# Tensor product of a graph network layer: VectorE's work on the pack before moved between the product groups of a pack's second step, and the index loads issued one turn earlier

## The chip, the core and the metric

The kernel runs on one core of a Trainium2 chip. That core has TensorE (PE in the profile, its weight loads PEld), VectorE (DVE), ScalarE (ACT), GpSimd (POOL) and SyncE (SP), which run side by side and wait for each other by semaphores. The metric is the device time of one execution in microseconds. Three runs of the kernel before took 8627.51, 8630.15 and 8634.26 us; the median is 8630.15.

## The reference

A two-layer graph network on 12,500 nodes with 32 features and 400,000 edges, sorted by their destination. The first layer is an attention over the edges, the second a tensor product:

```
h = max(layernorm(x), 0)
x = x + attention(h)                       # layer 0: q, k, v of 4 heads, softmax over a node's edges
h = max(layernorm(x), 0)                   # 8 scalars and 8 vectors per node
R = relu(weight * w1 + b1) @ w2 + b2       # per edge: 384 radial weights
Y = spherical_harmonics(edge_attr)         # per edge
msg[e, o] = sum over u, v, i: R[e, u, v, k] * Y[e, f] * h[src[e], v, i] * C[o, f, i]
x = x + (h + sum of msg over the edges of each destination)
```

Everything here concerns `msg` and the sum over edges. For it an edge's source row `h[src]` is gathered, its vectors are turned into a frame along the edge, multiplied by the radial weights and summed over the 16 inputs, and turned back.

## The kernel before

The edges are padded to 128 x 3132: each of the 128 partitions holds 3132 edges ("slots") in order. The tensor product (`tensor_product`) works on packs of 18 slots, 174 packs in all; 3 packs are a chunk, 6 packs (two chunks) are one pass of the loop body, and a pack is one *turn* `j` of it. Each engine has its own instruction stream, written out by hand in its function; there is no scheduler. What stands in these streams, and the semaphores, set the order.

For each pack:

- GpSimd gathers the 18 source rows of each partition with 18 indirect DMAs (`feat<-scratch_h,src`, line 993) into one of three buffers. At a pack's start it waits for `feat_free`, which VectorE counts up once it has used the rows, and at a chunk's start for the index list `src_i[b]`, which ACT loads (line 1123).
- VectorE *rotates* the vectors (line 1209, three instructions) and forms the *operands* (line 1218, three).
- TensorE computes the radial weights in six *weight groups*, of three slots each (lines 1008 and 1009, six matmuls a group, `radial`), into two alternating PSUM buffers `psR`. Group g waits until VectorE's product of group g - 2 is done (line 1005's wait on `prod_done`), because it overwrites its buffer.
- VectorE multiplies a group by the operands (line 1241, three instructions a group, the *product*). Products 0 to 2 are a pack's first step, 3 to 5 its second. Behind each step stands a *fold* (line 1250) that adds a few of the 16 inputs, so that TensorE has fewer to sum.
- TensorE sums a step's products over the inputs with an identity matrix (lines 1020 and 1023, the *sum*). The last matmuls of a sum (line 1023) wait for the fold.
- ACT evicts the sum from PSUM into `red` (line 1082), and prepares seeds, flags and frames (lines 1089, 1091, 1059).
- VectorE, one turn later, does the *rotations back* (line 1258, three), *additions back* (copy of line 1267, additions of lines 1269 and 1270) and *scans* (line 1279, four), which run the sums along the edges of a node. ACT stores the result (lines 1098 and 1100).

TensorE's queue is, for a pack: groups 2, 3, 4, 5; first sum; groups 0 and 1 of the next pack; second sum. It works through it in order, so group 5, which waits for product 3, holds up the first sum behind it.

VectorE's queue in a turn is: products 0 to 2, fold, products 3 to 5, fold, rotations back, additions back, scans (of the pack before), rotate, operands (of the pack behind).

Of the kernel before, what the change touches and what calls it, by code (L numbers as in the profile page):

```python
# [883 lines left out]
def tensor_product(nc, a, k):  # L884
# [11 lines left out]
    with ExitStack() as ctx:  # L896
# [41 lines left out]
        with nc.Block(no_gpsimd_drain=True) as block:  # L938
# [107 lines left out]
            def _(act):  # L1046
# [61 lines left out]
                def body(i, first, last):  # L1108
                    for j in range(TURN):
# [11 lines left out]
                        if j % PACKS == PACKS - 1 and not last:  # L1121
                            b = j // PACKS
                            act.dma_start(src_i[b][:, :], sources[:, bass.ds(i * (2 * T) + (b + 2) * T, T)]).then_inc(src_loaded[b], 16)
# [12 lines left out]
            def _(vec):  # L1136
# [87 lines left out]
                def products(i, j, s, first):  # L1224

                    q = i * (TURN * SPP) + j * SPP + s
                    r = (j * SPP + s) % 2
                    if not (first and j == 0):
                        vec.wait_ge(sum_ready, q - 1)
                    if s == 0:  # L1230
                        vec.wait_ge(turned_ready, i * TURN + j + 1)
                    for third in range(GROUPS):
                        g = GROUPS * s + third
                        ts = slice(g * TRI, (g + 1) * TRI)
                        vec.wait_ge(radial_ready, i * (TURN * GPP) + j * GPP + g + 1)
                        to = prod[r][:, third * TRI:(third + 1) * TRI, :, :]
                        for lo, n, frm in ((0, 2 * VU, 0), (2 * VU, VU, 256), (3 * VU, VU, 256)):
                            x = max(0, lo // VU - 1)
                            if s == 0 and third == 0 and x == 1:
                                vec.wait_ge(turned_copied, i * (TURN * 2) + j * 2 + 2)  # L1240
                            v.tensor_tensor(to[:, :, :, lo:lo + n], psR[:, g % 2, :, frm:frm + n * JC].rearrange("p t (j u) -> p t j u", j=JC),  # L1241
                                            ops[j % 2][:, ts, x * JC:(x + 1) * JC].rearrange("p t (j o) -> p t j o", o=1).to_broadcast([P, TRI, JC, n]),
                                            ALU.mult).then_inc(prod_done, 1)
# [42 lines left out]
                def body(i, first, last):  # L1286
                    step = chain(vec, vec_done, base + i * (TURN * per_pack) - (0 if first else of_finish))
                    for j in range(TURN):
                        begun, more = not (first and j == 0), not (last and j == TURN - 1)
                        products(i, j, 0, first)  # L1290
                        fold(i, j, 0)
                        products(i, j, 1, first)
                        fold(i, j, 1)
                        if begun:
                            rotate_back(step, i, j - 1, 0 if more else 1)
                            add_back(step, i, j - 1)
                            scan(step, i, j - 1)
                        if more:
# [151 lines left out]
```

## Time and profile before

| | |
|---|---|
| median of three runs | 8630.15 us |
| the profiled execution's own time | 8642.33 us |
| its span, first to last instruction | 8640.3 us |
| PE busy | 3594.6 us (42%) |
| DVE busy | 5311.7 us (61%) |
| POOL busy | 6479.9 us (75%) |
| ACT busy | 1921.1 us (22%) |
| first and last start of the tensor product's gathers | 4409.2 and 8465.1 us |

Times are those of one profiled execution. The share of busy time is over the whole span, of which the tensor product is a little under half; in the other half TensorE hardly works.
### The profile page before, as it was taken

How to read it: one execution, taken by the hardware profiler on the slowest of the kernel's cores; microseconds unless marked ns; L12 is line 12 of the kernel's file. 1: busy time of each engine (PE TensorE's matmuls, PEld its weight loads, DVE VectorE, ACT ScalarE, POOL GpSimd, SP SyncE). 2: the span in 40 equal slices, each digit the busy share in tenths (PEclk: the TensorE clock that was granted, in tenths of full speed). 3: DMA queues.
4: the chain of work that ended last, by engine and by line, in shares of the span. 5: the costliest groups of instructions: out<-in, count | busy, mean ns of one | idle time of the engine just before them, and what ended most of it. 6: DMA issues, size and time to landing. Idle time of an engine off the chain costs nothing. (4 is left out here: it accounts for less than half of the span.)

```text
span 8640.3 us, 61009 instructions
## 1 busy us (share of the span) xinstructions
PE 3594.6 (42%) x15884; PEld 2458.9 (28%) x15884; DVE 5311.7 (61%) x7917; ACT 1921.1 (22%) x2576; POOL 6479.9 (75%) x6677
## 2 busy tenths in 40 slices
PE   1000000000000000000048888888888888888882
PEld 0000000000000000000035655556555656655651
DVE  3233333343333433334369999999999999999993
ACT  0123332223322233222201111111111111111110
POOL 7777777777777777777667777777777777777775
PEclk6555555555555555555579999999999999999996
DMA  7333444334443444443222222222222222222221
GB/s 301 102 107 109 116 113 122 107 109 114 113 124 107 110 112 114 122 111 110 63 52 70 68 66 67 69 68 66 67 70 68 66 68 70 66 68 66 70 66 29
DMA packets 364374, 796.10 MB, mean 92 GB/s; under 512 B 143582, under 2 KB 209998, under 8 KB 344638
## 3 DMA queue, kind: packets, MB, share of 16 engines
q1 hardware_dynamic: 99880, 491.45, 19.3%
q0 software_dynamic: 213216, 166.16, 10.3%
q10 hardware_dynamic: 51126, 136.22, 4.2%
q8 instruction: 125, 2.05, 0.1%
q14 instruction: 27, 0.22, 0.0%
HBM read 499.72 MB, written 293.61 MB: 92 GB/s over the span
## 5 line engine op out<-in xcount | busy, mean ns | idle before, releaser
L993 POOL DMA_INDIRECT feat<-scratch_h,src x3132 | 3102.2, 990 | 975.1 <-issue 954.7
L537 POOL DMA_INDIRECT kv<-scratch_kv,src_i x3132 | 2971.9, 949 | 959.8 <-issue 959.8
L1020 PE MATMUL psS<-prod,ident 128*128 128x288 f32 x7656 | 1986.2, 417 | 0.7 <-ACT red L1082 0.7
L1241 DVE TENSOR_TENSOR prod<-psR,ops 128x384 f32<-128x384 f32 (+1 forms) x3132 | 1919.6, 682 | 82.7 <-PE psR L1009 47.3
L804 PE MATMUL psA<-ident,tail 128*36 128x128 f32 x3 | 0.8, 413 | 3936.5 <-DVEq L829 3936.5
L1020 PEld LDWEIGHTS psS<-prod,ident 128*128 128x128 f32 x7656 | 1505.0, 198 | 423.4 <-issue 14.1
L1008 PE MATMUL psR<-whigh,stack 128*128 128x384 f16 x3132 | 1066.8, 341 | 540.7 <-DVE prod L1241 531.1
L804 PEld LDWEIGHTS psA<-ident,tail 128*36 128x36 f32 x3 | 0.3, 127 | 3936.7 <-DVEq L829 3936.6
L1009 PE MATMUL psR<-wlow,capped 128*128 128x384 f16 x3132 | 1067.7, 342 | 0.0
L689 DVE TENSOR_TENSOR qk<-psQ,kv 128x1728 f32<-128x1728 f32 x58 | 113.6, 1958 | 1473.7 <-DMA kv<-scratch_kv,src_i 1473.7
L1082 ACT ACTIVATE red<-psS,scales 128x288 f32<-128x288 f32 x348 | 174.6, 502 | 2388.7 <-PE psS L1023 2388.3
L674 DVE TENSOR_TENSOR_SCAN psQ<-psQ,qseed 128x1760 f32<-128x1760 f32 x58 | 222.2, 3832 | 591.6 <-ACT qseed L566 591.6
L1008 PEld LDWEIGHTS psR<-whigh,stack 128*128 128x128 f16 x3132 | 312.8, 100 | 938.3 <-DVE prod L1241 753.0
L1023 PE MATMUL psS<-prod,ident 128*128 128x288 f32 x1740 | 478.9, 406 | 0.0
L1209 DVE TENSOR_TENSOR parts<-feat,psF 128x432 f32<-128x432 f32 x519 | 282.4, 599 | 173.1 <-DMA feat<-scratch_h,src 173.1
L585 ACT ACTIVATE psD<-decay 128x1980 f32<-128x1980 f32 x58 | 107.4, 1851 | 1205.2 <-DVEq L700 1205.2
L1009 PEld LDWEIGHTS psR<-wlow,capped 128*128 128x128 f16 x3132 | 316.4, 101 | 202.6 <-issue 25.4
L682 DVE TENSOR_TENSOR low<-psD,high 128x1728 f16<-128x1728 f32 x116 | 227.1, 1958 | 216.1 <-ACT high L577 203.3
L1023 PEld LDWEIGHTS psS<-prod,ident 128*128 128x128 f32 x1740 | 330.6, 190 | 91.3
L1218 DVE TENSOR_REDUCE ops<-parts 128x144 f32<-128x432 f32 x522 | 306.1, 642 | 42.1 <-DVE parts L1209 42.1
L592 ACT ACTIVATE out<-sums 128x1944 f32<-128x1944 f32 x58 | 219.9, 3792 | 468.4 <-DVEq L708 468.4
L1250 DVE TENSOR_TENSOR prod<-prod 128x864 f32<-128x864 f32 x348 | 316.1, 908 | 11.9
(254 smaller groups left out, 4039.3 us busy)
## 6 DMA issues: line engine op xcount, KB each, us to landing
w_row<-in_wT SPq DMA_DIRECT2D x116, 864.0 KB
stack<-scratch_hid SPq DMA_DIRECT2D x174, 576.0 KB
scratch_state<-out ACTq DMA_DIRECT2D x58, 1080.0 KB
kv<-scratch_kv,src_i POOLq DMA_INDIRECT x3132
qin<-scratch_qexp SPq DMA_DIRECT2D x58, 864.0 KB, 4.5
scratch_hid<-high SPq DMA_DIRECT2D x116, 432.0 KB, 11.1
scratch_hid<-low SPq DMA_DIRECT2D x116, 432.0 KB, 12.0
feat<-scratch_h,src POOLq DMA_INDIRECT x3132
```

Source lines behind the costliest of these rows:

```text
L537: nc.gpsimd.indirect_dma_start(kv[b][:, t, :], None, a["kv"], bass.IndirectOffsetOnAxis(ap=src_i[b][:, t:t + 1].bitcast(U32), axis=0)).the ...
L674: step(v.tensor_tensor_scan(flat(qrun), flat(qrun), flat(qseed), 0.0, ALU.mult, ALU.add))
L682: v.tensor_tensor(low[:, cols], units, high[:, cols], ALU.subtract).then_inc(split_done, 1)
L993: nc.gpsimd.indirect_dma_start(feat[h][:, t, :], None, a["h2"], bass.IndirectOffsetOnAxis(ap=src_i[b][:, h * PACK + t:h * PACK + t + 1].bi ...
L1008: nc.tensor.matmul(psR[:, g % 2, t, 0:384], stack[:, slot, at:at + P], whigh[:, :], start=True, stop=False)
L1009: last_mm = nc.tensor.matmul(psR[:, g % 2, t, 0:384], capped[:, slot, at:at + P], wlow[:, :], start=False, stop=True)
L1020: nc.tensor.matmul(into, ident[:, :], prod[r][:, :, j, :], start=(n == 0), stop=False)
L1023: last_mm = nc.tensor.matmul(into, ident[:, :], prod[r][:, :, j, :], start=False, stop=(j == FOLDS[s] - 1))
L1209: step(v.tensor_tensor(parts[:, :, n, :].rearrange("p t (i u) -> p t i u", i=3), f[:, :, VU:D].rearrange("p t (i u) -> p t i u", i=3), at[ ...
L1218: add_up = lambda n: v.tensor_reduce(ops[j % 2][:, :, n * JC + VU:(n + 1) * JC], parts[:, :, n, :].rearrange("p t (i u) -> p t u i", i=3), ...
L1241: v.tensor_tensor(to[:, :, :, lo:lo + n], psR[:, g % 2, :, frm:frm + n * JC].rearrange("p t (j u) -> p t j u", j=JC), ops[j % 2][:, ts, x ...
L1250: v.tensor_tensor(prod[r][:, :, 0:FOLDS[s], :], prod[r][:, :, 0:FOLDS[s], :], prod[r][:, :, JC // 2:JC // 2 + FOLDS[s], :], ALU.add).then_ ...
```

## The change

The function `products`, which did a step's three products, becomes `product` for one group; its waits and instructions are the same. In VectorE's turn the work for the pack before no longer stands behind the second fold as one block. Rotations back stand between the first fold and product 3, additions back between products 3 and 4, scans between 4 and 5, and rotate comes ahead of the second fold, with the operands behind it. On ACT the load of the next index list is issued in the turn `j % 3 == 1` of a chunk in place of `j % 3 == 2`.

```diff
-                        if j % PACKS == PACKS - 1 and not last:
+                        if j % PACKS == PACKS - 2 and not last:
                             b = j // PACKS
                             act.dma_start(src_i[b][:, :], sources[:, bass.ds(i * (2 * T) + (b + 2) * T, T)]).then_inc(src_loaded[b], 16)
...
-                def products(i, j, s, first):
+                def product(i, j, g, first):
...
+                    s, third = g // GROUPS, g % GROUPS
...
-                        products(i, j, 0, first)
+                        for g in range(GROUPS):
+                            product(i, j, g, first)
                         fold(i, j, 0)
-                        products(i, j, 1, first)
-                        fold(i, j, 1)
                         if begun:
                             rotate_back(step, i, j - 1, 0 if more else 1)
+                        product(i, j, GROUPS, first)
+                        if begun:
                             add_back(step, i, j - 1)
+                        product(i, j, GROUPS + 1, first)
+                        if begun:
                             scan(step, i, j - 1)
+                        product(i, j, GROUPS + 2, first)
                         if more:
                             rotate(step, i, j + 1)
+                        fold(i, j, 1)
+                        if more:
                             operands(step, i, j + 1)
```

VectorE's queue in one turn, before, from the first fold on (9x96 is the first fold, 9x64 the second; a product is a row of 48x16 and one of 48x8 x2; `back` are the rotations back, `seed` and `run` additions back and scans):

```order
L1250 TENSOR_TENSOR prod<-prod 128x9x96 [waits prod_done]
L1241 TENSOR_TENSOR prod<-psR,ops 128x48x16 [waits radial_ready,sum_ready]
L1241 TENSOR_TENSOR prod<-psR,ops 128x48x8 x2
L1241 TENSOR_TENSOR prod<-psR,ops 128x48x16 [waits radial_ready]
L1241 TENSOR_TENSOR prod<-psR,ops 128x48x8 x2
L1241 TENSOR_TENSOR prod<-psR,ops 128x48x16 [waits radial_ready]
L1241 TENSOR_TENSOR prod<-psR,ops 128x48x8 x2
L1250 TENSOR_TENSOR prod<-prod 128x9x64 [waits prod_done]
L1258 TENSOR_TENSOR back<-red,psF 128x18x24 [waits flags_ready4,frames_ready4,sum_free]
L1258 TENSOR_TENSOR back<-red,psF 128x18x24 x2
L1267 COPY seed<-run 128x32 [waits vec_done4,scanned]
```

The same place of VectorE's queue in the changed kernel, where line numbers from 1226 on are one lower:

```order
L1249 TENSOR_TENSOR prod<-prod 128x9x96 [waits prod_done]
L1257 TENSOR_TENSOR back<-red,psF 128x18x24 [waits flags_ready4,frames_ready4,sum_free]
L1257 TENSOR_TENSOR back<-red,psF 128x18x24 x2
L1240 TENSOR_TENSOR prod<-psR,ops 128x48x16 [waits radial_ready,sum_ready]
L1240 TENSOR_TENSOR prod<-psR,ops 128x48x8 x2
L1266 COPY seed<-run 128x32 [waits vec_done4,scanned]
L1268 TENSOR_TENSOR seed<-back 128x24x18
L1269 TENSOR_TENSOR seed<-seed,back 128x24x18 [waits vec_done4]
L1240 TENSOR_TENSOR prod<-psR,ops 128x48x16 [waits radial_ready]
L1240 TENSOR_TENSOR prod<-psR,ops 128x48x8 x2
L1278 SCALAR_TENSOR_TENSOR run<-psF,seed 128x152 [waits run_copied,seeded,vec_done4]
L1278 SCALAR_TENSOR_TENSOR run<-psF,seed 128x152 x3
```

Three rotations back have come between the first fold and product 3, and additions and scans between the products behind it.

The end of a turn in VectorE's queue, before (the scans, then `parts` for rotate and `ops` for the operands):

```order
L1279 SCALAR_TENSOR_TENSOR run<-psF,seed 128x152 [waits run_copied,seeded,vec_done4]
L1279 SCALAR_TENSOR_TENSOR run<-psF,seed 128x152 x3
L1209 TENSOR_TENSOR parts<-feat,psF 128x18x24 [waits feat_here1,frames_ready4]
L1209 TENSOR_TENSOR parts<-feat,psF 128x18x24 x2
L1218 TENSOR_REDUCE ops<-parts 128x18x8 [waits vec_done4,ops_copied]
L1218 TENSOR_REDUCE ops<-parts 128x18x8 x2
```

And in the changed kernel, from product 5 on:

```order
L1240 TENSOR_TENSOR prod<-psR,ops 128x48x16 [waits radial_ready]
L1240 TENSOR_TENSOR prod<-psR,ops 128x48x8 x2
L1209 TENSOR_TENSOR parts<-feat,psF 128x18x24 [waits feat_here1,frames_ready4]
L1209 TENSOR_TENSOR parts<-feat,psF 128x18x24 x2
L1249 TENSOR_TENSOR prod<-prod 128x9x64 [waits prod_done]
L1218 TENSOR_REDUCE ops<-parts 128x18x8 [waits vec_done4,ops_copied]
L1218 TENSOR_REDUCE ops<-parts 128x18x8 x2
```

The second fold now stands behind rotate, and so behind its wait for the gathered rows. The orders of TensorE, GpSimd and SP in this stage stay as they were.

ACT's queue, the difference at one index load:

```order
 L1068 ACTIVATE ops<-feat 128x18x8 [waits ops_free,feat_here2]
+L1123 DMA src_0<-in_src 128x54
 L1074 ACTIVATE ops<-ops 128x18x8 [waits turned_ready]
 L1075 ACTIVATE ops<-ops 128x18x8
...
 L1068 ACTIVATE ops<-feat 128x18x8 [waits ops_free,feat_here0]
-L1123 DMA src_0<-in_src 128x54
 L1074 ACTIVATE ops<-ops 128x18x8 [waits turned_ready]
```

The load has moved one turn up, behind the scalars of the chunk's last pack.

## Rows read from the trace of the kernel before

**Rows 1.** Page: busy (share); granted clock in 40 slices; a group: busy, mean, idle.
```profile
...
PE 3594.6 (42%) x15884; PEld 2458.9 (28%) x15884; DVE 5311.7 (61%) x7917; ACT 1921.1 (22%) x2576; POOL 6479.9 (75%) x6677
...
PEclk6555555555555555555579999999999999999996
...
L993 POOL DMA_INDIRECT feat<-scratch_h,src x3132 | 3102.2, 990 | 975.1 <-issue 954.7
...
```

**Rows 2.** Line 993: ns min/median/max, first and last start.
```profile
...
L993 POOL DMA_INDIRECT feat<-scratch_h,src x3132: 943/947/1819, 4409.2 to 8465.1; - x196
...
```

**Rows 3.** Timeline of VectorE, one turn: start, us, line, names, count, idle before.
```profile
...
6000.58 3.68 DVE L1241 TENSOR_TENSOR prod<-psR,ops 128x768 f32<-128x768 f32 x6 [0.20 <-DVE ops L1218]
6004.75 1.89 DVE L1241 TENSOR_TENSOR prod<-psR,ops 128x768 f32<-128x768 f32 x3 [0.48 <-PE psR L1009]
6006.67 1.06 DVE L1250 TENSOR_TENSOR prod<-prod 128x864 f32<-128x864 f32 x1
6007.65 5.46 DVE L1241 TENSOR_TENSOR prod<-psR,ops 128x768 f32<-128x768 f32 x9
6013.15 0.76 DVE L1250 TENSOR_TENSOR prod<-prod 128x576 f32<-128x576 f32 x1
6013.82 1.63 DVE L1258 TENSOR_TENSOR back<-red,psF 128x432 f32<-128x432 f32 x3
6015.68 0.41 DVE L1267 COPY seed<-run 128x32 f32<-128x32 f32 x1 [0.23 <-DVE back L1258]
6015.78 0.94 DVE L1269 TENSOR_TENSOR seed<-back 128x432 f32<-128x432 f32 x1
...
6017.74 1.57 DVE L1279 TENSOR_TENSOR_SCAN run<-psF,seed 128x152 f32<-128x152 f32 x4
6020.23 1.64 DVE L1209 TENSOR_TENSOR parts<-feat,psF 128x432 f32<-128x432 f32 x3 [0.92 <-DMA feat<-scratch_h,src]
6022.11 1.76 DVE L1218 TENSOR_REDUCE ops<-parts 128x144 f32<-128x432 f32 x3 [0.24 <-DVE parts L1209]
```

**Rows 4.** Timeline of TensorE, the same turn and the sum ahead of it.
```profile
...
5996.78 5.98 PE L1020 MATMUL psS<-prod,ident 128*128 128x288 f32 x24
...
6003.57 0.33 PE L1008 MATMUL psR<-whigh,stack 128*128 128x384 f16 x1
...
6009.58 0.34 PE L1008 MATMUL psR<-whigh,stack 128*128 128x384 f16 x1 [1.74 <-DVE prod L1241]
...
6016.87 0.33 PE L1008 MATMUL psR<-whigh,stack 128*128 128x384 f16 x1
...
6018.82 0.41 PE L1020 MATMUL psS<-prod,ident 128*128 128x288 f32 x1
```

**Rows 5.** Stretches: busy time of each engine, granted clock, DMA share, GB/s.
```profile
...
4440.00:8400.00 3960.00, 3446.57 (x15287) 2360.76 (x15286) 3606.12 (x6105) 697.18 (x1691) 3027.84 (x3058) 0.96 0.27 68
5984.00:5990.00 6.00, 4.26 (x14) 2.80 (x14) 5.84 (x11) 0.00 (x0) 4.61 (x5) 0.72 0.34 93
6007.00:6010.50 3.50, 1.76 (x12) 0.89 (x10) 3.50 (x6) 0.00 (x0) 2.89 (x3) 1.00 0.29 94
...
```

**Rows 6.** Timeline of TensorE, the turn before.
```profile
...
5985.86 0.34 PE L1008 MATMUL psR<-whigh,stack 128*128 128x384 f16 x1 [1.74 <-DVE prod L1241]
...
5986.19 0.52 PE L1008 MATMUL psR<-whigh,stack 128*128 128x384 f16 x1
...
5994.83 0.33 PE L1008 MATMUL psR<-whigh,stack 128*128 128x384 f16 x1
...
```

**Rows 7.** Timeline of ACT.
```profile
...
6026.79 0.28 ACT L1091 ACTIVATE psF<-same_all 128x144 f32 x1
...
```

**Rows 8.** Waits, 6000 to 6500 us: us in total, times, longest.
```profile
...
ACT red L1082 <- PE psS L1023: 286.5, 43, 13.5
...
```

**Rows 9.** Timeline of GpSimd.
```profile
...
6006.87 1.69 POOL L993 DMA_INDIRECT feat<-scratch_h,src  x1 [0.30 <-issue]
...
6016.37 1.18 POOL L993 DMA_INDIRECT feat<-scratch_h,src  x1 [0.30 <-issue]
...
```

More of the change, by code:

```diff
@@ L1222, in operands @@
                     add_up(2).then_inc(turned_ready, 1)
-                def products(i, j, s, first):
+                def product(i, j, g, first):
+                    s, third = g // GROUPS, g % GROUPS
                     q = i * (TURN * SPP) + j * SPP + s
                     r = (j * SPP + s) % 2
-                    if not (first and j == 0):
+                    if third == 0 and not (first and j == 0):
                         vec.wait_ge(sum_ready, q - 1)
-                    if s == 0:
+                    if g == 0:
@@ L1231, in products @@
                         vec.wait_ge(turned_ready, i * TURN + j + 1)
[L1232 to L1243, printed above, removed]
+                    ts = slice(g * TRI, (g + 1) * TRI)
@@ new lines, in product @@
+                    vec.wait_ge(radial_ready, i * (TURN * GPP) + j * GPP + g + 1)
+                    to = prod[r][:, third * TRI:(third + 1) * TRI, :, :]
+                    for lo, n, frm in ((0, 2 * VU, 0), (2 * VU, VU, 256), (3 * VU, VU, 256)):
+                        x = max(0, lo // VU - 1)
+                        if g == 0 and x == 1:
+                            vec.wait_ge(turned_copied, i * (TURN * 2) + j * 2 + 2)
+                        v.tensor_tensor(to[:, :, :, lo:lo + n], psR[:, g % 2, :, frm:frm + n * JC].rearrange("p t (j u) -> p t j u", j=JC),
+                                        ops[j % 2][:, ts, x * JC:(x + 1) * JC].rearrange("p t (j o) -> p t j o", o=1).to_broadcast([P, TRI, JC, n]),
+                                        ALU.mult).then_inc(prod_done, 1)
```

## The prediction

> **What bounds the kernel now.** I read the busy line and the clock row of the page first [rows 1]. The reader should see two stages: one to about half of the span, in which PE is hardly used at all, and the tensor product behind it, the only stage that the change touches. Then the gathers of line 993 [rows 1, 2]: the first starts at 4409.2 and the last at 8465.1 us, 3132 of them, and nearly all idle time between them (954.7 us, 0.305 us each) is "issue". So GpSimd waits for nobody in the whole stage. It issues 18 gathers a pack; (8465.1 - 4409.2) / 3132 = 1.295 us each, 23.31 us a pack, and there are 174 packs. VectorE's timeline shows the same from the other side [rows 3]: at 6020.23 it waits 0.92 us for the last gather of the next pack. GpSimd sets the pace.
>
> How near are the others? VectorE and TensorE make a loop with each other. TensorE's rows of one turn [rows 4] and VectorE's [rows 3] give it, from the start of the last weight group of a pack (group 5) round to the same in the next:
> - group 5 and the 26 matmul records of the first sum: 6009.58 to 6016.87, 7.29 us
> - groups 0 and 1 of the next pack: 6016.87 to 6018.82, 1.95
> - the 28 records of the second sum: 5996.78 to 6003.57, 6.79 (TensorE has no wait in it)
> - group 2 until VectorE starts its product: 6003.57 to 6004.75, 1.18
> - that product: to 6006.67, 1.92
> - first fold until the next product: to 6007.65, 0.98
> - product 3 until group 5 starts: to 6009.58, 1.93.
> Together 22.04 us, 1.28 under the 23.31 of GpSimd. That is all the slack there is.
>
> A part of it is eaten already. In the turn before, the granted clock is 0.72 over six microseconds [rows 5], a mix of the levels 2.4 and 1.2 GHz; the fall comes right behind the idle time of 1.74 us ahead of group 5, and the same stretch (group 5 to group 0) takes 5985.86 to 5994.83 = 8.97 us and not 7.29 [rows 6]. A fall costs TensorE 1.68 us, more than the slack, and so VectorE waits 0.48 us for group 2 in the next turn [rows 3]. Over the stage the mean granted clock is 0.96 [rows 5]: 0.04 x 3960 us = 158 us of full speed lost, by 1.68 us some 94 falls in 170 packs, about every second pack.
>
> **The change part by part.** Nothing is added or removed, and TensorE's own order stays as it is. Four things move.
>
> (1) *The three rotations back stand between the first fold and product 3.* They last 1.63 us [rows 3]. They lie now behind the second fold, off the loop; in the new place they lie in it, since group 5 waits for product 3 and the first sum stands behind group 5 in TensorE's queue. Loop: 22.04 + 1.63 = 23.67 us. Could the rotations wait as well, for ACT's flags? The flags end at 6027.07 [rows 7], 1.46 us after the second sum (6018.82 + 6.79 = 6025.61); the loop gives them 1.18 + 1.92 + 0.98 = 4.08 us. No wait.
>
> (2) *Additions back ahead of product 4, scans ahead of product 5.* After product 3 VectorE needs 2.06 us for copy and additions (6015.68 to 6017.74), 1.82 for product 4, 1.6 for the scans, 1.82 for product 5: 7.3 us. TensorE is in group 5 and the first sum for 7.29, and groups 0 and 1 come behind it with 0.98 each. Group 1, which waits for product 5, can start at 8.3 at the earliest anyway. So this work lies beside the first sum, as the matmuls cover it; without that cover it would be on the loop with its full length. The settling waits of 0.23 ahead of the copy go, because product 3 stands between; they were in VectorE's own time, which isn't the bound, so 0.
>
> (3) *Second fold behind rotate.* It is 0.76 us, needed by the last 4 of 28 records of the second sum. It can start 1.64 us after the next pack's rows land, some 2 to 3 us after product 5, when TensorE has about 5 us of that sum left. 0. Behind it the operands start 0.7 us later in VectorE's queue, products 0 to 2 with them. From the end of product 5 VectorE needs 1.64 + 0.7 + 1.76 + 0.2 + 3.68 = 8.0 us to stand ready for product 2; TensorE needs, from the same moment, 1.07 to the start of group 1, then 0.98 + 6.79 + 1.18: 10.0. VectorE waits, not TensorE: 0.
>
> (4) *Index loads a turn earlier on ACT.* Two issues of about 0.3 us in six turns, on a queue that idles 286.5 us of 500 for the sums alone [rows 8]. GpSimd didn't wait for them before [rows 1]. 0, where it is the bound or where it is not.
>
> So without the clock a pack goes from 23.31 to 23.67. Now the clock. Until now TensorE idles at most 1.74 us in a row ahead of group 5 [rows 4, 6]; now the wait between group 4 (0.98 long, starting when product 2 ends) and group 5 lasts 0.98 + 1.63 + 1.82 = 4.43 less 0.98, about 3.5 us, with only one group in the 5.6 us ahead of group 5. If every second pack has a fall behind 1.74 us of idle, I take one for each pack behind 3.5. The price has two ends. At the low one falls stay as frequent as now, 94 x 1.68 / 170 = 0.93 us a pack. At the high one each pack has a fall wholly in work, and some a second: 1.9 us (all of it 1.68, and a sixth more). A fall that begins in the idle time costs less than the full 1.68, and half of the low clock's time may lie there in some packs; so I take 1.4, the middle. And now nothing hides it: the loop is the bound. Sum: 23.67 + 1.4, some 25.05 us a pack, 1.73 more than now (25.05 - 23.32). The rotations back stand in 173 turns: +299 us. What stands behind the last gather keeps its work and changes by one wait: I take 0, with 3 us to each side.
>
> From the profiled execution: its span 8640.3, own time 8642.3; 8642.3 + 299 = 8941. The median of the runs shown is 12.2 us under the profiled one: 8929, rounded to **8930 us**, 3.5% slower. With the bounds of the clock: 23.67 + 0.93 = 24.60, +1.29 x 173 = 223, 8853; and 25.57, +2.26 x 173 = 391, 9021. The loop's terms have been read in one turn and may be off by 0.2 us in all, 35 us.
>
> The Trainium skill says in "TensorE: Matmul & The Clock Gate", section "What's actually happening", that the clock is granted by how busy the engine has been recently. The rows show that for one place only (clock 0.72 behind the idle time, 1.00 in the next turn [rows 5]); it would make the change dearer, in the direction that I take.
>
> **GpSimd after the change.** It has to stay under 25.05. The median gather takes 947 ns and the mean 990 [rows 1, 2]: 0.04 x 18 = 0.8 us a pack is delay, and 22.5 is the least. The delay sits on single gathers. That of 6006.87 takes 1.69 us while the first fold (6006.67 to 7.73) is on [rows 3, 9], that of 6016.37 takes 1.18 beside the addition of line 1269 (to 6016.72); both end 0.83 us after VectorE's instruction does. Beside scans or rotations they take 0.94 to 0.95. If they were met by chance, windows of 1.06, 0.76 and 1.9 us against a gather each 1.25 us would cost about 1.06 x 1.06 / 2.5 + 0.76 x 0.76 / 2.5 + 0.56 = 1.24 us (a window squared, by twice the 1.25; the 0.56 is for the two additions, of which a gather is caught by one: 0.94 x 0.94 / 2.5 = 0.35, and 0.31 / 1.25 x 0.83 = 0.21). Then a pack takes GpSimd 23.75 us, under 25.05: hidden.
> The Trainium skill, "SBUF — State Buffer", section "SBUF: two separate sides", says that VectorE and GpSimd share a port pair as an exclusive lock, taken by a VectorE instruction with two SBUF inputs for its whole length. The rows agree: folds and additions have both inputs in SBUF, rotations and products one in PSUM. It speaks for the view that moving folds can slow gathers; by that alone a pack would go from 23.31 to 23.75, +0.44 x 173 = 76 us, a rival below.
>
> **Rivals.**
> A: *The loop binds, but the clock hardly falls*, because falls need what the old place had. 23.67, perhaps 23.8 with GpSimd's delays: +62 to +85 us, about 8700. Against: TensorE's quiet stretch gets longer, and the fall is seen behind a shorter one.
> B: *GpSimd stays the bound and is hit more often*: 8630 + 76 = 8706. For: it paces now. Against: it needs the loop to be under 23.8.
> C: *Faster.* Folds and additions now lie apart; as VectorE waits for the gathers, they always meet them at the same phase, and that may be a good one. Without delay a pack is 22.5 us: -0.78 x 173 = -135, 8495. It decides only if the loop is at most 22.5, so if group 5 does not wait for the rotations back; that would need product 3 to be no condition of it. Against: the count of product instructions that group 5 waits for reaches product 3.
> D: *No change*: the phase is as before and the loop stays within the slack; 8630. The 1.63 us in 1.28 of slack speak against it.
>
> **Chances.** Forecast 0.82 (its own range 8820 to 9025), A 0.06, B 0.04, C 0.04, D 0.04. The range 8800 to 9025 leaves out A to D, 0.18, and takes in the bounds of the clock with the 35 us at the lower end. A measurement of this kernel tells no less than 0.2% (17 us) from no change. Faster 0.04, same 0.04, slower 0.92.
>
> **What would show it.** In the new profile: gathers with idle time for a semaphore, not only "issue", and a mean pace of about 25 us a pack; the wait of rotate for the gathers gone, and VectorE waiting about a microsecond or two for group 2 in nearly each turn; TensorE's wait ahead of group 5 some 3.5 us; the mean granted clock of the stage down, to about 0.92 to 0.94. It would be wrong if the gathers still run without a wait (B, C or D), if group 5 starts before the rotations back have run (C), or if the clock stays at 0.96 with a pack under 24 us (A).

## The result, and the profile after

The changed kernel takes 9032.22 us (median of 4 runs, 9030.99 to 9032.77) against 8631.71 of the kernel before (4 runs); the ratio is 1.0461, 95% interval 1.0448 to 1.0474. It is slower, as forecast, but by 400 us and not by 299: 9032 lies 7 us above the range, which ended at 9025.

The page of the changed kernel: busy time, granted clock in 40 slices, and two groups (busy, mean ns, idle before and what ended most of it).

```profile
...
PE 3772.1 (42%) x15884; PEld 2588.9 (29%) x15884; DVE 5241.6 (58%) x7917; ACT 1900.9 (21%) x2576; POOL 6403.3 (71%) x6677
...
PEclk6555555555555555555689898998989989899896
...
L993 POOL DMA_INDIRECT feat<-scratch_h,src x3132 | 3031.8, 968 | 1383.4 <-issue 909.7
...
L1240 DVE TENSOR_TENSOR prod<-psR,ops 128x384 f32<-128x384 f32 (+1 forms) x3132 | 1944.0, 680 | 580.2 <-PE psR L1009 548.8
...
```

The products on the page of the kernel before:

```profile
...
L1241 DVE TENSOR_TENSOR prod<-psR,ops 128x384 f32<-128x384 f32 (+1 forms) x3132 | 1919.6, 682 | 82.7 <-PE psR L1009 47.3
...
```

Against [rows 1] the clock row, which read 9 all through the tensor product, now goes up and down between 8 and 9, and VectorE's products (line 1240) wait 548.8 us for the weight groups, where they waited 47.3. The gathers themselves have become shorter, 968 ns in the mean after 990.

Line 993 in the changed kernel, which answers to [rows 2], with what ended the idle time before it:

```profile
...
L993 POOL DMA_INDIRECT feat<-scratch_h,src x3132: 938/944/1717, 4402.9 to 8796.9; - x196
...
  issue: 909.7, 2985
  DVEq L1217: 453.5, 146
...
```

In place of 4409.2 to 8465.1 us the gathers now run to 8796.9, and in 146 of the 174 packs GpSimd waits for VectorE to give a buffer free (`DVEq L1217`). It no longer sets the pace.

TensorE's timeline over two turns, which answers to [rows 4, 6]:

```profile
...
5998.90 0.50 PE L1008 MATMUL psR<-whigh,stack 128*128 128x384 f16 x1 [3.28 <-DVE prod L1240]
...
6008.78 0.33 PE L1008 MATMUL psR<-whigh,stack 128*128 128x384 f16 x1
...
6010.73 5.98 PE L1020 MATMUL psS<-prod,ident 128*128 128x288 f32 x24
...
6017.52 0.33 PE L1008 MATMUL psR<-whigh,stack 128*128 128x384 f16 x1
...
6025.07 0.50 PE L1008 MATMUL psR<-whigh,stack 128*128 128x384 f16 x1 [3.28 <-DVE prod L1240]
...
6033.82 0.33 PE L1008 MATMUL psR<-whigh,stack 128*128 128x384 f16 x1
...
6050.10 0.50 PE L1008 MATMUL psR<-whigh,stack 128*128 128x384 f16 x1 [3.28 <-DVE prod L1240]
...
```

The rows with 3.28 us of idle time ahead are group 5 of three packs; it was 1.74. From one group 5 to the next it takes 26.17 us (5998.90 to 6025.07), and then 25.03. The second sum is 6.79 us as before (6010.73 to 6017.52). The stretch from group 5 to group 0 is 9.88 us in the first turn and 8.75 in the second; at the full clock it is 7.29.

VectorE's timeline of the first of these turns, from the second fold on, answers to [rows 3]:

```profile
...
6007.27 0.76 DVE L1249 TENSOR_TENSOR prod<-prod 128x576 f32<-128x576 f32 x1
6009.85 1.76 DVE L1218 TENSOR_REDUCE ops<-parts 128x144 f32<-128x432 f32 x3 [1.82 <-ACT ops L1068]
6011.80 3.68 DVE L1240 TENSOR_TENSOR prod<-psR,ops 128x768 f32<-128x768 f32 x6 [0.20 <-DVE ops L1218]
6018.69 1.89 DVE L1240 TENSOR_TENSOR prod<-psR,ops 128x768 f32<-128x768 f32 x3 [3.21 <-PE psR L1009]
6020.61 1.06 DVE L1249 TENSOR_TENSOR prod<-prod 128x864 f32<-128x864 f32 x1
6021.59 1.62 DVE L1257 TENSOR_TENSOR back<-red,psF 128x432 f32<-128x432 f32 x3
6023.13 1.88 DVE L1240 TENSOR_TENSOR prod<-psR,ops 128x768 f32<-128x768 f32 x3
6024.93 0.29 DVE L1266 COPY seed<-run 128x32 f32<-128x32 f32 x1
...
6030.13 1.85 DVE L1240 TENSOR_TENSOR prod<-psR,ops 128x768 f32<-128x768 f32 x3
6031.90 1.61 DVE L1209 TENSOR_TENSOR parts<-feat,psF 128x432 f32<-128x432 f32 x3
...
```

VectorE waits 3.21 us for group 2; between the fold at 6020.61 and product 3 at 6023.13 now stand the rotations back (6021.59). Rotate (6031.90) has no idle time for gathered rows any more, where it had 0.92. The operands at 6009.85 wait 1.82 us for ACT's copy, which stands behind the eviction of the late first sum; that is off the loop, since VectorE waits longer than that for group 2 all the same.

Stretches of the changed kernel, with the granted clock in the column before last but one; they answer to [rows 5]:

```profile
...
5999.00:6005.00 6.00, 6.00 (x17) 4.00 (x18) 5.96 (x12) 0.00 (x0) 4.47 (x6) 0.57 0.51 146
6025.00:6029.00 4.00, 3.93 (x13) 2.60 (x14) 3.97 (x8) 0.00 (x0) 3.08 (x4) 0.62 0.19 29
4440.00:8800.00 4360.00, 3630.61 (x15340) 2496.47 (x15339) 3553.21 (x6131) 681.60 (x1701) 3003.34 (x3103) 0.90 0.25 62
...
```

Right behind the 3.28 us of idle time the clock is 0.57 and 0.62, a mix of 2.4 and 1.2 GHz with most of it at the low level; over the stage its mean is 0.90 after 0.96.

The two turns stand for the stage: between 4500 and 8300 us all 148 stretches from group 5 to group 0 are longer than 8.6 us. Half of them last 9.8 to 9.9 us and half 8.7 to 8.8, by turns, and from one group 5 to the next it takes 25.60 us in the mean.

The sum of a turn in these rows: 7.29 for group 5 and first sum at full clock, then 1.95, 6.79, 1.17, 1.92, 0.98, 1.54 for the rotations back and 1.94 = 23.58 us; and for the clock 9.88 - 7.29 = 2.59 and 8.75 - 7.29 = 1.46, 2.03 in the mean. Together 25.6 us; 173 x (25.60 - 23.31) = 396 us. What is left stands at the end: the last rotations back wait for the last sum, 6.84 us before the change and 11.35 after it.

```profile
...
8496.14 1.63 DVE L1258 TENSOR_TENSOR back<-red,psF 128x432 f32<-128x432 f32 x3 [6.84 <-ACT psF L1091]
...
```

```profile
...
8885.17 1.63 DVE L1257 TENSOR_TENSOR back<-red,psF 128x432 f32<-128x432 f32 x3 [11.35 <-ACT psF L1091]
...
```

The first row is of the kernel before, the second of the changed one. 396 + 4.5 = 400.7 us; measured are 400.5. That they agree so closely is partly luck. All terms come from the two profiled executions, and these differ by 389 us (8642.33 and 9030.99): the one of the kernel before ran 10.6 us over its median, and its first gather started 6.3 us later (4409.2 and 4402.9). The sum is good to some ten us.

### The profile page after: what moved, and what is told of

Same layout as the page of the kernel before. It is cut to its first block and busy times, and to the rows that moved or that the text cites. A ratio compares the mean times of both kernels' runs of the same rounds, so it can differ in the third digit from the quotient of the medians.

```text
span 9029.2 us, 61171 instructions
## 1 busy us (share of the span) xinstructions
PE 3772.1 (42%) x15884; PEld 2588.9 (29%) x15884; DVE 5241.6 (58%) x7917; ACT 1900.9 (21%) x2576; POOL 6403.3 (71%) x6677
## 5 line engine op out<-in xcount | busy, mean ns | idle before, releaser
L993 POOL DMA_INDIRECT feat<-scratch_h,src x3132 | 3031.8, 968 | 1383.4 <-issue 909.7
L1240 DVE TENSOR_TENSOR prod<-psR,ops 128x384 f32<-128x384 f32 (+1 forms) x3132 | 1944.0, 680 | 580.2 <-PE psR L1009 548.8
L1020 PE MATMUL psS<-prod,ident 128*128 128x288 f32 x7656 | 2105.7, 435 | 0.7 <-ACT red L1082 0.7
L1020 PEld LDWEIGHTS psS<-prod,ident 128*128 128x128 f32 x7656 | 1594.1, 209 | 477.4 <-issue 29.3
L1008 PE MATMUL psR<-whigh,stack 128*128 128x384 f16 x3132 | 1122.8, 359 | 759.0 <-DVE prod L1240 750.7
L1009 PE MATMUL psR<-wlow,capped 128*128 128x384 f16 x3132 | 1125.5, 360 | 0.0
L1023 PE MATMUL psS<-prod,ident 128*128 128x288 f32 x1740 | 478.9, 406 | 0.0
L1023 PEld LDWEIGHTS psS<-prod,ident 128*128 128x128 f32 x1740 | 330.7, 190 | 91.3
L1257 DVE TENSOR_TENSOR back<-red,psF 128x432 f32<-128x432 f32 x522 | 282.5, 595 | 11.3 <-ACT psF L1091 11.3
```

Of the source, the lines that this page charges most:

```text
L993: nc.gpsimd.indirect_dma_start(feat[h][:, t, :], None, a["h2"], bass.IndirectOffsetOnAxis(ap=src_i[b][:, h * PACK + t:h * PACK + t + 1].bi ...
L1008: nc.tensor.matmul(psR[:, g % 2, t, 0:384], stack[:, slot, at:at + P], whigh[:, :], start=True, stop=False)
L1009: last_mm = nc.tensor.matmul(psR[:, g % 2, t, 0:384], capped[:, slot, at:at + P], wlow[:, :], start=False, stop=True)
L1020: nc.tensor.matmul(into, ident[:, :], prod[r][:, :, j, :], start=(n == 0), stop=False)
L1023: last_mm = nc.tensor.matmul(into, ident[:, :], prod[r][:, :, j, :], start=False, stop=(j == FOLDS[s] - 1))
L1257: step(v.tensor_tensor(back[:, :, n, :].rearrange("p t (o u) -> p t o u", o=3), red[j % 2][:, :, (n + 1) * VU:(n + 2) * VU].rearrange("p t ...
```

## The experiments

In the comparisons below the kernel before, run beside them on the same chip, took 8634.6 to 8635.0 us in the median. Ten runs, told last in this section, were measured on chips where it took over 10600 us.

### Only the rotations back moved

```diff
 fold(i, j, 0)
+if begun:
+    rotate_back(step, i, j - 1, 0 if more else 1)
 products(i, j, 1, first)
 fold(i, j, 1)
 if begun:
-    rotate_back(step, i, j - 1, 0 if more else 1)
     add_back(step, i, j - 1)
```

> The kernel before with only the three rotations back moved, between the first fold and product 3; additions, scans, rotate, second fold and index loads stay where they were. Theory: this one move is the whole loss, 25.0 to 25.6 us a pack, 8930 to 9035 us, and VectorE waits some 2 to 3 us for group 2. Rival (the rest of the change costs something of its own): clearly under 8930, the difference to 9032 being the share of the rest.

Measured: 9034.14 us, ratio 1.0461 (1.0443 to 1.0478), the same as the whole change within 2 us. Its gathers:

```profile
...
L993 POOL DMA_INDIRECT feat<-scratch_h,src x3132 | 3156.5, 1008 | 1260.8 <-issue 915.0
...
```

They are 40 ns longer in the mean than in the changed kernel (968), 0.7 us a pack, and it costs nothing, because GpSimd waits. So the rotations back alone are the loss; additions, scans, fold, rotate and index loads, as they stand in the change, cost and give nothing beside it.

### The rotations back taken out of the loop again

```diff
 fold(i, j, 0)
+product(i, j, GROUPS, first)
 if begun:
     rotate_back(step, i, j - 1, 0 if more else 1)
-product(i, j, GROUPS, first)
 if begun:
     add_back(step, i, j - 1)
```

> The changed kernel with one step undone in part: the three rotations back stand behind product 3 and not ahead of it; all else as changed. Theory (the loop of TensorE and VectorE goes through product 3, group 5 and the first sum, and 1.63 us of rotations back were put into it): the loop is back at 22.04 us, GpSimd sets the pace again, and a pack takes 22.5 us plus what folds and additions delay the gathers, 0.8 to 1.6 us: 23.3 to 24.1 us a pack, 8630 to 8770 us; mean granted clock of the stage 0.95 or more; no waits of GpSimd but issue. Rival (the cost lies in the second fold behind rotate, or in additions and scans between the products): it stays at 25.0 to 25.6 us a pack, 8930 to 9035 us.

Measured: 8703.12 us, 1.0078 (1.0062 to 1.0095). One exchange of two steps gives back 329 of the 400 us. The mean clock of the stage is 0.97, and the gathers read:

```profile
...
L993 POOL DMA_INDIRECT feat<-scratch_h,src x3132 | 3164.9, 1011 | 974.5 <-issue 954.2
...
```

GpSimd waits for nothing but "issue" again. The 68 us over the kernel before are in the gathers: (1011 - 990) ns x 3132 = 66 us.

### TensorE's idle time filled

```diff
 for g in range(...):
+    if g % GPP == GPP - 1:
+        pe.wait_ge(sum_free, i * (2 * SPP) + s + 2)
+        for _ in range(13):
+            nc.tensor.matmul(psS[:, 384:512], ident[:, :], ident[:, :], start=True, stop=True)
     if not last or g < 2 * GPP:
         radial(i, g)
```

> The changed kernel with 13 more matmuls of 128 columns ahead of group 5 of every pack, in TensorE's idle time of 3.3 us, written to unused columns of psS; they are not used by anything. Each takes about 0.21 us by the rate of the sums, 2.8 us in all, less than the idle time. Theory (1.93 us of the 25.60 us a pack are the lower granted clock that follows that idle time): the mean granted clock rises from 0.90 to 0.97 or more and a pack takes 23.7 to 23.9 us, some 8700 to 8740 us. Rival (the loop is that long by its waits, and the clock is a side effect): the clock rises and the time stays within 30 us of 9032. If the 13 take longer than the idle time, group 5 starts later and the gain is smaller by 173 times that.

Measured: 8689.01 us, 1.006 (1.0043 to 1.0077), 343 us under the changed kernel, though VectorE's order is that of the change. TensorE ahead of group 5, the clock of the stage, and the gathers:

```profile
...
6000.10 0.34 PE L1008 MATMUL psR<-whigh,stack 128*128 128x384 f16 x1 [1.00 <-DVE prod L1244]
...
6001.09 3.06 PE L1042 MATMUL psS<-ident 128*128 128x128 f32 x26
6004.53 0.34 PE L1008 MATMUL psR<-whigh,stack 128*128 128x384 f16 x1 [0.38 <-DVE prod L1244]
...
```

```profile
...
4440.00:8300.00 3860.00, 3636.21 (x18976) 2710.82 (x18975) 3407.93 (x5878) 671.34 (x1630) 2962.46 (x2945) 1.00 0.27 67
...
```

```profile
...
L993 POOL DMA_INDIRECT feat<-scratch_h,src x3132 | 3151.4, 1006 | 975.1 <-issue 954.5
...
```

The 13 matmuls (26 records, 3.06 us) leave 0.38 us idle, and the clock is 1.00. Without its falls the loop is 23.58 us, which is just what GpSimd takes here: 18 x (1.006 + 0.305) = 23.60, and it doesn't wait. Which of the two keeps the kernel 54 us over the one before, this run can't tell, since they come out alike. But the 1.63 us of rotations by themselves cost no more than these 54 us; the other 343 are the lower clock that the longer idle time brings. The rival, the clock as a side effect only, is out.

The same with 6 matmuls in place of 13:

> The changed kernel with 6 matmuls of 128 columns in the idle time ahead of group 5; the last attempt, for the same reason. Theory (how often the clock falls goes by how long TensorE is idle there): mean clock 0.94 to 0.97, 24.2 to 24.6 us a pack, 8785 to 8855 us where the kernel before takes 8635. Rival (any filler keeps the clock up): 8690. Rival 2 (only a closed gap does): 9030.

Measured: 8736.27 us, 1.0118 (1.0101 to 1.0135): faster than expected. TensorE ahead of group 5, and the clock of the stage:

```profile
...
6037.90 1.50 PE L1042 MATMUL psS<-ident 128*128 128x128 f32 x12
6041.35 0.34 PE L1008 MATMUL psR<-whigh,stack 128*128 128x384 f16 x1 [1.95 <-DVE prod L1244]
...
```

```profile
...
4440.00:8300.00 3860.00, 3383.96 (x16476) 2456.64 (x16475) 3359.82 (x5811) 646.75 (x1615) 2933.26 (x2943) 0.99 0.26 66
...
```

The idle time is 1.95 us, longer than the 1.74 of the kernel before, and yet the clock is 0.99 and not 0.96. The step from "how long TensorE idles in a row" to "how often the clock falls" was wrong: here 1.5 us of filler stand between group 4 and group 5, just ahead of the idle time. That this work kept the clock up fits the run; none here changes the work and leaves the idle time as it is. What 8736 is made of: 173 x (T - 23.31) = 101 us gives T = 23.9, and that is the loop, 23.58, plus 0.3 for the few falls left.

### The same filler in the kernel before

5 matmuls ahead of group 5, the same edit in the kernel before.

> The kernel before with 5 more matmuls of 128 columns ahead of group 5, in the idle time of 1.74 us (0.24 us each, 1.2 us together); where the kernel before takes over 10000 us the run says nothing. Theory (GpSimd sets the pace of the kernel before; what the lower clock costs TensorE there, 1.68 us in every second pack, ends in a wait of VectorE and not in the time): the clock goes from 0.96 to 0.99 or 1.00, VectorE's waits for group 2 shrink, and the time changes only by how the gathers now meet folds and additions: 23.0 to 23.5 us a pack, 8580 to 8665 us, in step with the mean gather. Rival (the clock is on the path before as well): -40 us with the mean gather at 990 ns as before.

Measured: 8578.82 us, 0.9935 (0.9919 to 0.9952). Clock of the stage, and gathers:

```profile
...
4440.00:8300.00 3860.00, 3487.73 (x16793) 2462.63 (x16794) 3551.82 (x6038) 689.04 (x1672) 2938.17 (x3024) 1.00 0.27 69
...
```

```profile
...
L993 POOL DMA_INDIRECT feat<-scratch_h,src x3132 | 3042.5, 971 | 975.1 <-issue 954.7
...
```

The clock has gone to 1.00, and the time went by what the gathers did: (990 - 971) ns x 3132 = 60 us, measured 56. GpSimd never waits. VectorE no longer stands still for 0.48 us in some turns, and its folds meet the gathers at other places. The rival wanted 40 us at an unchanged mean gather; the gathers account for all of it.

### The first fold behind product 3 as well

```diff
+product(i, j, GROUPS, first)
 fold(i, j, 0)
 if begun:
     rotate_back(step, i, j - 1, 0 if more else 1)
-product(i, j, GROUPS, first)
```

> The changed kernel with the first fold and the rotations back behind product 3: products 0 to 3, first fold, rotations back, additions back, product 4, scans, product 5, rotate, second fold, operands. Theory: neither the fold (0.98 us) nor the rotations back are in the loop any more, 22.04 - 0.98 = 21.1 us; TensorE waits less than 1 us ahead of group 5, so the clock does not fall there; GpSimd sets the pace, and the gathers meet folds and additions at other places. A walk through one turn with the durations of the rows gives 0.35 to 0.5 us of delay a pack in place of 0.8: 22.9 to 23.0 us, 8545 to 8580 us, under the kernel before. Rival (delays of the gathers are by chance, 1.24 us a pack): 23.75 us a pack, about 8705 us. Rival 2 (the loop is not what was slow): 8930 or more.

Measured: 8511.15 us, 0.9854 (0.9838 to 0.987). It beats both kernels, the one before by 124 us. Group 5 and the gathers:

```profile
...
6022.63 0.34 PE L1008 MATMUL psR<-whigh,stack 128*128 128x384 f16 x1 [0.64 <-DVE prod L1240]
...
```

```profile
...
L993 POOL DMA_INDIRECT feat<-scratch_h,src x3132 | 2974.0, 950 | 974.5 <-issue 954.2
...
```

TensorE idles 0.64 us ahead of group 5, the clock of the stage is 1.00. The gathers are at 950 ns in the mean, so near their 945 that a pack takes 18 x (0.950 + 0.305) = 22.59 us; there is hardly anything left to win here as long as 3132 gathers are issued one by one. It came out lower than expected (22.9 to 23.0 us), and (990 - 950) ns x 3132 = 125 us is the whole of the gain.

Is that the shorter loop, or where the fold meets the gathers? In the next run rotations back and fold are exchanged, so that the two together end when they did:

```diff
 product(i, j, GROUPS, first)
-fold(i, j, 0)
 if begun:
     rotate_back(step, i, j - 1, 0 if more else 1)
+fold(i, j, 0)
```

> The kernel with first fold and rotations back behind product 3, these two exchanged: the rotations back first, then the fold; the last attempt at it, since in the calls before the kernel before itself took over 10600 us. Theory (what is left over 22.5 us a pack is gathers held up by a fold or an addition that VectorE runs at that moment, so it goes by their phase): the mean gather between 985 and 1010 ns, 8610 to 8710 us where the kernel before takes 8635. Rival (it was the shorter loop that made the time 8511): unchanged, within 10 us. Where the kernel before takes over 10000 us again, the run says nothing on it.

Measured: 8633.19 us, 1.0 (0.999 to 1.0009). The clock is 1.00 over the stage, as in the kernel of 8511 us, and GpSimd waits for nothing but "issue" in both. The gathers, one of them (GpSimd's timeline), and what VectorE runs beside it (its timeline):

```profile
...
L993 POOL DMA_INDIRECT feat<-scratch_h,src x3132 | 3097.6, 989 | 974.5 <-issue 954.2
...
```

```profile
...
6025.94 1.65 POOL L993 DMA_INDIRECT feat<-scratch_h,src  x1 [0.30 <-issue]
...
```

```profile
...
6025.81 0.95 DVE L1269 TENSOR_TENSOR seed<-seed,back 128x432 f32<-128x432 f32 x1
...
```

The gather that starts at 6025.94 falls into the addition that ends at 6026.76, and ends 0.83 us after it, at 6027.59. It is so in nearly each turn: 165 gathers start inside this addition here, and they take 1.53 us or more; in the kernel of 8511 us none does. There the gather meets the first fold in another way (GpSimd's and VectorE's timelines of that kernel):

```profile
...
6022.50 0.94 POOL L993 DMA_INDIRECT feat<-scratch_h,src  x1 [0.30 <-issue]
...
```

```profile
...
6022.49 1.09 DVE L1249 TENSOR_TENSOR prod<-prod 128x864 f32<-128x864 f32 x1
...
```

They start together, within 0.06 us, in 127 of the 174 turns. The gather then isn't held up, and the fold takes up to 1.11 us, where it takes 1.04 to 1.05 elsewhere in this kernel. With the exchange the whole kernel is 122 us slower for 39 ns x 3132 = 122 us of longer gathers. The phase decides, not the loop.

### Only the index loads moved

```diff
-if j % PACKS == PACKS - 1 and not last:
+if j % PACKS == PACKS - 2 and not last:
```

> The kernel before with only the index loads issued a turn earlier. Both theories expect no change: GpSimd never waited for them, 8635 us within 15. Where the kernel before takes over 10000 us the run says nothing.

Measured: 8632.51 us, 0.9998 (0.9989 to 1.0008). They are worth nothing here.

### Ten runs that tell nothing on the change

The kernels of *half filled* (6 matmuls), *back ahead of fold*, *before filled* and *index loads only* were first measured on three chips on which the kernel before itself took 10783, 10652 and 10665 us. TensorE, VectorE and ACT had waits of several microseconds there that no other trace here has, and GpSimd waited for VectorE in 161 to 170 packs, so the pace was another; why, no run shows. Their edits are those shown above. On the first of these chips:

> The kernel before with only the index loads issued a turn earlier. Both theories expect no change: GpSimd never waited for them, 8635 us within 15. A difference would show that the loads' place matters while GpSimd sets the pace.

10848.72 us, 1.0053 (1.0036 to 1.0071).

> The kernel before with 5 more matmuls of 128 columns ahead of group 5, in the idle time of 1.74 us (0.24 us each, 1.2 us together); nothing uses them. Theory (GpSimd sets the pace there; the lower clock behind that idle time costs TensorE 1.68 us in every second pack, and VectorE's wait for group 2 is all that comes of it): the clock goes from 0.96 to 0.99 or 1.00, VectorE's waits for group 2 go, and the time changes only by how the gathers now meet folds and additions, 23.0 to 23.5 us a pack, 8580 to 8665 us. Rival (the clock is on the path before as well): 0.48 us in every second pack come back, 40 us, whatever the gathers do, and the mean gather stays at 990 ns.

10942.25 us, 1.0169 (1.0143 to 1.0195).

> The changed kernel with 6 matmuls in the idle time ahead of group 5 in place of 13: 1.4 us of 3.3 filled, 1.9 us left, about what the kernel before has (1.74). Theory (how often the clock falls goes by how long TensorE is idle there): falls in about every second pack, mean clock 0.94 to 0.97, and as the loop has no slack each costs its time: 23.7 + 0.5 to 0.9 us a pack, 24.2 to 24.6, 8785 to 8855 us. Rival (any filler keeps the clock up): 8690, as with 13. Rival 2 (only a closed gap does): 9030.

10836.28 us, 1.0066 (1.0042 to 1.009).

> The kernel with first fold and rotations back behind product 3, these two exchanged: the rotations back first, then the fold. The fold starts 1.63 us later and nothing else changes its time; the loop has 21.1 us in both, the clock stays at 1.00, the same instructions run. Theory (what is left over 22.5 us a pack is gathers held up by a fold or an addition that VectorE runs at that moment, so it goes by their phase): the mean gather rises from 950 to between 990 and 1010 ns, 23.2 to 23.7 us a pack, 8625 to 8710 us. Rival (it was the shorter loop that made the time 8511): unchanged, within 10 us.

10771.52 us, 0.9992 (0.9977 to 1.0007).

On the second:

> The changed kernel with 6 matmuls of 128 columns in the idle time ahead of group 5 in place of 13: 1.4 us of 3.3 filled, 1.9 us left, about what the kernel before has (1.74). Once more, as in the call before the kernel before itself took 10783 us. Theory (how often the clock falls goes by how long TensorE is idle there): falls in about every second pack, mean clock 0.94 to 0.97, and as the loop has no slack each costs its time: 24.2 to 24.6 us a pack, 8785 to 8855 us. Rival (any filler keeps the clock up): 8690, as with 13. Rival 2 (only a closed gap does): 9030.

10498.83 us, 0.9854 (0.9836 to 0.9873).

> The kernel with first fold and rotations back behind product 3, these two exchanged: the rotations back first, then the fold. Once more, as in the call before the kernel before itself took 10783 us. The fold starts 1.63 us later, nothing else changes its place; the loop has 21.1 us in both, the clock stays at 1.00, the same instructions run. Theory (what is left over 22.5 us a pack is gathers held up by a fold or an addition that VectorE runs at that moment, so it goes by their phase): the mean gather rises from 950 to between 985 and 1010 ns, 23.1 to 23.7 us a pack, 8610 to 8710 us. Rival (it was the shorter loop that made the time 8511): unchanged, within 10 us.

10439.36 us, 0.9812 (0.9787 to 0.9837).

> The kernel before with 5 more matmuls of 128 columns ahead of group 5, in the idle time of 1.74 us (0.24 us each, 1.2 us together). Once more, as in the call before the kernel before itself took 10783 us. Theory (GpSimd sets the pace; the lower clock behind that idle time costs TensorE 1.68 us in every second pack, and VectorE's wait for group 2 is all that comes of it): the clock goes from 0.96 to 0.99 or 1.00, VectorE's waits for group 2 shrink, and the time changes only by how the gathers now meet folds and additions: 23.0 to 23.5 us a pack, 8580 to 8665 us. Rival (the clock is on the path before as well): the waits of 0.48 us in every second pack come back, -40 us, with the mean gather at 990 ns as before.

10701.52 us, 1.0047 (1.0032 to 1.0061).

> The kernel before with only the index loads issued a turn earlier. Once more, as in the call before the kernel before itself took 10783 us. Both theories expect no change: GpSimd never waited for them, 8635 us within 15.

10697.84 us, 1.0043 (1.0028 to 1.0058).

On the third:

> The changed kernel with 6 matmuls of 128 columns in the idle time ahead of group 5: 1.4 us of 3.3 filled, 1.9 us left, about what the kernel before has (1.74). In the two calls before, the kernel before itself took 10652 and 10783 us, with waits in the timelines that are not in its trace here; so once more. Theory (how often the clock falls goes by how long TensorE is idle there): falls in about every second pack, mean clock 0.94 to 0.97, and as the loop has no slack each costs its time: 24.2 to 24.6 us a pack, 8785 to 8855 us. Rival (any filler keeps the clock up): 8690, as with 13. Rival 2 (only a closed gap does): 9030.

10525.0 us, 0.9865 (0.9837 to 0.9893).

> The kernel with first fold and rotations back behind product 3, these two exchanged: the rotations back first, then the fold. Once more, for the same reason. The fold starts 1.63 us later, nothing else changes its place; the loop has 21.1 us in both, the clock stays at 1.00, the same instructions run. Theory (what is left over 22.5 us a pack is gathers held up by a fold or an addition that VectorE runs at that moment, so it goes by their phase): the mean gather rises from 950 to between 985 and 1010 ns, 23.1 to 23.7 us a pack, 8610 to 8710 us. Rival (it was the shorter loop that made the time 8511): unchanged, within 10 us.

10478.86 us, 0.9842 (0.9809 to 0.9875).

The same kernel (half filled) has ratios of 0.9865 and 1.0066 on different ones of them; no verdict rests on these runs.

## Why the prediction was off

*What bounds the kernel.* Right. GpSimd paced the kernel before, and the loop of TensorE and VectorE had 1.28 us of slack. The six other kernels in which GpSimd never waits differ by their gathers alone: 21, 16, -1, -1, -19 and -40 ns of mean gather against the 990 of before make 66, 50, -3, -3, -60 and -125 us of 3132 gathers; measured are 68, 54, -1, -2, -56 and -124.

*Rotations back in the loop.* Right in place and nearly in size: 1.54 us in the rows after the change, 1.63 taken. The run with these alone moved gives the whole loss.

*Additions, scans, second fold, operands, index loads at nothing.* Right: 9034 us without them and 9032 with them, and 8632.5 for the index loads. They are not without effect as such: the run that keeps them and puts the rotations back behind product 3 is 68 us slower than the kernel before, by longer gathers. In the changed kernel this is covered by GpSimd's wait, as the prediction had it.

*The clock.* This is the step that failed, in its size: the prediction took 1.4 us a pack and 1.9 as its high end, and the rows have 2.03 (2.59 and 1.46 in turn). How often it falls was right, once in each turn. The mistake was the price: at most 1.68 us each, as one fall had cost in the kernel before. In every second turn the clock stays low for longer, so that 2.59 us go; why it alternates, no run shows. With 2.59 us a pack as the high end the range would have held the result. With 2.03 the same sum gives 173 x (23.67 + 2.03 - 23.32) = 412, less 16 for the rotations at 1.54 and more 4.5 for the tail, 400. The signs point the same way: VectorE waits 3.21 us for group 2 where one or two were expected, and the clock is 0.90 and not 0.92 to 0.94. The expectation, held later, that falls go by the idle time alone was refuted by the half-filled run.

*The arithmetic.* Small slips, each of which pulled the forecast or its high end down: 23.67 + 1.4 is 25.07 and not 25.05, 1.68 and a sixth more is 1.96 and not 1.9 (9032 us in place of 9021), and the 35 us for terms read in a single turn were added at the low end of the range alone; at the high end they would have made it 9056. Without these slips the range would have held the result, but the term of 1.4 us would have been short all the same, by 0.63 us a pack, about 109 us.

*The end.* Taken as 0 with 3 us to each side, it is 4.5 us.

*GpSimd after the change.* Right: gathers stay under the loop and wait. The rule of the Trainium skill ("SBUF — State Buffer", section "SBUF: two separate sides") that an instruction of VectorE with two SBUF inputs takes a port pair that it shares with GpSimd, and keeps it to its end against a GpSimd operation that reads SBUF, fits the long gathers of the stage: they end 0.82 to 0.83 us after a fold or an addition, and those that start beside rotations or scans take 0.94. The runs show the phase and the price; that it is a port is the page's reading, and no run here took the second SBUF input away. Nor does one show why a gather that starts together with the fold gets through in 0.94 us. Two inputs are not the only case: ahead of the first pack the gather that starts at 4420.44 us in the kernel before, inside a cast of the weights with one input (line 1188, from 4420.35, 0.36 us long), takes 1.09 us.

Rivals: A needed a clock that hardly falls (0.90 speaks against it); it is what the filled run makes, 8689 us where the prediction had about 8700. B, C and D needed gathers that never wait. C, the good phase, exists, at 8511 us, in the one order tried here that has product 3 ahead of the fold and the fold ahead of the rotations.

## What to carry to other kernels

Before work is moved between two engines' steps, walk once round the loop in which they wait for each other and compare it with the engine that paces now: 1.63 us moved into 1.28 us of slack cost at most 54 us at the full clock, but the idle time that it opened on TensorE cost 343 us more in clock. A fall of the clock is to be priced by how long it lasts in the new place, not by what one cost in the old. An engine that issues without a wait for thousands of microseconds is the pace, and then look at the mean of its instruction against its median: here 43 ns of 990 were 135 us; the best order of another engine's steps won 124 of them back, and the exchange of two steps in it gave 122 away again.

## What the runs showed of the hardware

- Granted clock of the stage, with TensorE's idle time ahead of group 5: 0.90 at 3.28 us, 0.96 at 1.74, 0.99 at 1.95 with 1.5 us of other matmuls ahead of it, 1.00 at 0.38 with 3.06 us of them, and 1.00 at 0.64 in the kernel of 8511 us, whose longest idle time in a turn is mostly 1.43. Useless matmuls in a wait won 343 us.
- A gather issued by GpSimd takes 0.94 us, and up to 1.8 where it starts during an fp32 addition of VectorE whose inputs are both in SBUF; it then ends 0.82 to 0.83 us after that instruction. VectorE's instruction isn't longer for it: the first fold is 1.06 us with and without in the kernel before and the changed one.
- Where gather and fold start together (from 0.06 us before to 0.03 us behind the fold's start, 127 times in the kernel of 8511 us), the gather takes 0.94 to 0.96 us and it is the fold that is longer, up to 1.11 us for 1.05.
